# Layer 0 of a four-layer hybrid network: token transposes and affinity logits in one 100-column product per tile, copies interleaved with the norms

## The reference

```
x = x + L0_conv(gn(x))            # super-token attention, the subject here
x = x + L1_conv(gn(x))            # 6-head attention, head mixing, softmax, norm
t = tokens(x)
t = t + L2_attn(ln(t)); t = t + L2_ffn(ln(t))
t = t + L3_attn(ln(t)); t = t + L3_ffn(ln(t))    # four experts, top 2
```

```
stf = blocks.mean(axis=(3, 5))                      # super tokens: mean of a block
s9  = unfold9(stf)                                  # 9 neighbours, missing ones are 0
affinity = softmax(einsum('bnpc,bnck->bnpk', pix, s9) * C**-0.5)
s   = einsum('bnpc,bnpk->bnck', pix, affinity)
stf = fold9(s) / (aff_sum + 1e-12)                  # attention over stf, then out = s9 * affinity
```

## Time and profile before

| | |
|---|---|
| median of three runs | 793.6 us (792.63 to 794.2) |
| the profiled execution | 793.93 us, its span 791.8 us |
| PE, weight loads | 736.5 us busy (93%), 577.3 us (73%) |
| DVE, ACT, GpSimd | 580.7 us (73%), 570.9 us (72%), 252.8 us (32%) |
| chain that ended last | PE 74%, DVE 13%, ACT 4%, issue 4% |
| granted TensorE clock | mean 0.981 |
| DMA | 41.36 MB, mean 52 GB/s |

### The profile page before, as it was taken

One profiled execution on the slowest core, in us unless ns is written; L12 is line 12 of the kernel. 1 busy time (PEld: TensorE's weight loads), 2 busy tenths in 40 slices (PEclk: granted clock), 3 DMA queues, 4 the chain that ended last, 5 costly groups with the idle time before them and its releaser, 6 DMA issues.

```text
span 791.8 us, 16975 instructions
## 1 busy us (share of the span) xinstructions
PE 736.5 (93%) x5269; PEld 577.3 (73%) x5269; DVE 580.7 (73%) x1425; ACT 570.9 (72%) x1427; POOL 252.8 (32%) x485
## 2 busy tenths in 40 slices
PE   1899999999999889999998986999999999999997
PEld 1876878778788776777776585777777787777775
DVE  6245887767677566788886798688888836988885
ACT  2326777787777558888886866788888847777775
POOL 1902345556554432121212000121212111534434
PEclk9999999999999999999999999999999979999999
DMA  6000001011011132233330002233333102233220
GB/s 221 0 2 0 2 12 16 16 22 16 16 21 16 27 91 81 80 101 98 84 104 13 0 1 82 58 94 90 99 99 83 38 1 67 67 72 70 60 50 21
DMA packets 60073, 41.36 MB, mean 52 GB/s; under 512 B 33904, under 2 KB 52464, under 8 KB 59888
## 3 DMA queue, kind: packets, MB, share of 16 engines
q1 hardware_dynamic: 60016, 40.63, 20.3%
HBM read 12.24 MB, written 3.21 MB: 20 GB/s over the span
## 4 chain that ended last, share of the span: by engine, by line
PE 74%; DVE 13%; ACT 4%; issue 4%; DMA 2%; SPq 1%; POOL 1%; POOLq 0%; DVEq 0%
PE ps L1261 11%; PE ps L995 9%; PE ps L1443 9%; PE ps L1186 9%; PE ps L1096 6%; PE ps L1000 5%; PE ps L1080 3%; PE ps L1024 3%; PE ps L1038 2%; PE ps L1003 2%; PE ps L1025 2%; PE ps L945 2%; DVE amax L1902 2%; ACT ee L627 2%; PE ps L1068 2%
## 5 line engine op out<-in xcount | busy, mean ns | idle before, releaser
L627 ACT ACTIVATE ee<-ps,nmax 128x128 f32<-128x128 f32 (+1 forms) x576 | 204.6, 443 | 10.4 <-DVE nmax L1614 5.2
L1261 PE MATMUL ps<-w,ee 128*128 128x128 f32 x960 | 134.6, 273 | 2.0 <-ACT big L614 1.9
L1261 PEld LDWEIGHTS ps<-w,ee 128*128 128x128 f32 x960 | 112.2, 142 | 13.0 <-ACT ee L627 2.8
L614 ACT ACTIVATE big<-ps 128x512 f32<-128x512 f32 (+1 forms) x192 | 96.5, 555 | 22.3 <-PE ps L1261 20.6
L1617 DVE TENSOR_REDUCE nmax<-ps 128x2 f32<-128x256 f32 x192 | 97.4, 549 | 12.2 <-PE ps L1003 7.5
L1745 DVE TENSOR_TENSOR hhl<-ee,hhl 128x512 fp32r<-128x512 f32 x96 | 77.3, 814 | 26.3 <-ACT hhl L864 24.8
L995 PE MATMUL ps<-kh,big 128*128 128x256 f32 x384 | 92.9, 385 | 1.6 <-POOL big L387 1.2
L1614 DVE TENSOR_REDUCE nmax<-ps 128x4 f32<-128x1024 f32 x48 | 58.7, 1223 | 40.9 <-PE ps L995 40.8
L1443 PE MATMUL ps<-hhl,w2hl 128*96 128x512 f32 x288 | 83.3, 399 | 2.1 <-issue 1.8
L1186 PE MATMUL ps<-qk,w1hl 128*128 128x512 f32 x288 | 84.4, 402 | 0.0
L531 POOL TENSOR_TENSOR xc<-big,xc 96x512 f32<-96x512 f32 x32 | 53.0, 1657 | 95.7 <-DVE big L1987 95.2
(11 more groups left out here) (260 smaller groups left out, 1329.2 us busy)
## 6 DMA issues: line engine op xcount, KB each, us to landing
qk<-hl SPq DMA_DIRECT2D x256, 96.0 KB, 3.1
big<-moe_gate SPq DMA_DIRECT2D x8, 768.0 KB, 6.8
w<-w_in SPq DMA_DIRECT2D x1, 1735.0 KB, 12.1
xc<-x_in SPq DMA_DIRECT2D x4, 384.0 KB, 5.6
l_mix<-on SPq DMA_DIRECT2D x32, 48.0 KB, 2.1
tok<-l_mix SPq DMA_DIRECT2D x16, 96.0 KB, 2.0
out<-xc SPq DMA_DIRECT2D x8, 192.0 KB, 2.1
w<-w_in SPq DMA_DIRECT2D x1, 998.0 KB, 8.8
```

Source lines behind the costliest of these rows:

```text
L614: nc.scalar.activation(et[:, h, 0:w], ps[:, 4 + hh, 0:w], ACT.Copy).then_inc(own(l, f"et{hh}"), 1)
L627: last = nc.scalar.activation(ee[:, ke, hh, qc, 0:w], src, ACT.Exp, bias=nmax[:, kp, hh, qc:qc + 1])
L1261: last = nc.tensor.transpose(ps[:, 4 + hh, b * P:(b + 1) * P], ee[:, u, hh, qc, tc * P:(tc + 1) * P], ident)
```

## The change

The moving operand of a tile's product becomes a new buffer `idst`, which holds for each image 4 columns of `stf` and the 96 x 96 identity. One product of 100 columns (ordinary, no longer a transpose) gives logits and tokens side by side, and `l0_xt` holds for each tile a zero column, 4 logits, 96 channels and the one (102 columns for 97).

- ACT writes the 16 copies of the identity into `idst` in one instruction, ahead of `norm_root`; DVE's last step on the means writes the other columns.
- PE waits for both before its first tile, and runs the eight groups in a row; the 32 logit products are gone. Behind the groups stand 20 fills.
- ACT does copies 0 to 3 behind norms 9, 11, 13 and 15 (counted from 0) and copies 4 to 7 behind them; the exponentials come behind all copies.
- DVE waits for all eight copies. The maximum runs over 5 columns, the zero among them, in SBUF, so the maximum with 0 is gone; the subtraction reads the logits from SBUF.
- GpSimd writes the zero column, and its wait for `stf` moves behind the fifth of the nine memsets.

```diff
-            nc.gpsimd.memset(l0_xt[:, :, C:C + 1], 1.0).then_inc(sg("pool_ones"), 1)
+            nc.gpsimd.memset(l0_xt[:, :, 0:1], 0.0).then_inc(sg("l0_zero"), 1)
+            nc.gpsimd.memset(l0_xt[:, :, xw - 1:xw], 1.0).then_inc(sg("pool_ones"), 1)
...
-            pool.wait_ge(sg("l0_dve"), L0_DVE["l0_stf"])
...
                 pool.wait_ge(sg("zeroed"), START + n)
+                if n == 5:
+                    pool.wait_ge(sg("l0_dve"), L0_DVE["l0_stf"])
                 nc.gpsimd.memset(t, 0.0).then_inc(sg("zeroed"), 1)
...
+            act.wait_ge(sg("w128_loaded"), 16)
+            nc.scalar.activation(idst[:, :, M:M + C], mid_dim(wb("ident", C)[:, 0:C], 1, B), ACT.Copy).then_inc(sg("l0_idst"), 1)
             norm_root("gn0", C, 0, B)
...
             for i in range(B):
                 norm_image("gn0", i)
...
-            for g in range(2):
+                if i >= 9 and i % 2 == 1:
+                    tokens_to_sbuf((i - 9) // 2)
+            for g in range(4, 8):
                 tokens_to_sbuf(g)
             act.wait_ge(sg("l0_dve"), L0_DVE["l0_logit"])
...
-            for g in range(2, 8):
-                tokens_to_sbuf(g)
...
-                    last = nc.tensor.transpose(ps[:, 4 + g % 4, t * C:(t + 1) * C], xn[0:C, a:a + P], wb("ident", C)[:, 0:C])
+                    last = mm(ps[:, 4 + g % 4, t * (M + C):(t + 1) * (M + C)], xn[0:C, a:a + P], idst[:, (g * 4 + t) // TPI, :], start=True, stop=True)
...
-            for g in range(2):
+            pe.wait_ge(sg("l0_idst"), 1)
+            pe.wait_ge(sg("l0_dve"), L0_DVE["l0_stf"])
+            for g in range(8):
                 tokens(g)
-            pe.wait_ge(sg("l0_dve"), L0_DVE["l0_stf"])
-            for t in range(NT):
-                i = t // TPI
-                pe.wait_ge(sg("gn0_xn"), i + 1)
-                last = mm(ps[:, 1, t * M:(t + 1) * M], xn[0:C, t * P:(t + 1) * P], stf[:, i * M:(i + 1) * M], start=True, stop=True)
-            last.then_inc(sg("l0_ps"), 1)
-            for g in range(2, 8):
-                tokens(g)
+            fill(20)
...
-            dve.wait_ge(sg("l0_ps"), L0_PS["l0_logit_ps"])
-            lg = ps[:, 1, 0:NT * M].rearrange("p (t m) -> p t m", m=M)
-            link(V.tensor_reduce(out=st[:, 4, :], in_=lg, axis=AX.X, op=ALU.max))
-            link(V.tensor_scalar(st[:, 4, :], st[:, 4, :], 0.0, None, ALU.max))
-            V.tensor_tensor(a0[:, :, :], lg, last_dim(st[:, 4, :], M), ALU.subtract).then_inc(sg("l0_dve"), 1)
+            dve.wait_ge(sg("l0_xt"), 8)
+            dve.wait_ge(sg("l0_zero"), 1)
+            link(V.tensor_reduce(out=st[:, 4, :], in_=l0_xt[:, :, 0:1 + M], axis=AX.X, op=ALU.max))
+            V.tensor_tensor(a0[:, :, :], l0_xt[:, :, 1:1 + M], last_dim(st[:, 4, :], M), ALU.subtract).then_inc(sg("l0_dve"), 1)
```

More of the change, by code:

```diff
@@ L65 @@
 SUMS_AT = {"gn0": 0, "gn1a": 1, "gn1b": 7, "gn1c": 7}
-L0_PS = {"l0_logit_ps": 1, "l0_stok_ps": 2, "l0_stokt_ps": 3, "l0_qkv_ps": 4, "l0_sc_ps": 5, "l0_proj_ps": 6}
+L0_PS = {"l0_stok_ps": 1, "l0_stokt_ps": 2, "l0_qkv_ps": 3, "l0_sc_ps": 4, "l0_proj_ps": 5}
 L0_DVE = {"l0_stf": 1, "l0_logit": 2, "l0_bd": 3, "l0_stok": 4, "l0_stf1": 5, "l0_prod": 6, "l0_sc": 7, "l0_o": 8}
@@ L196, in hybrid_kernel @@
         bd_w = 2 * M * B + M
-        xt_w = NT * (C + 1)
-        l0_xt = big[:, 0:xt_w].rearrange("p (t c) -> p t c", c=C + 1)
+        xw = 1 + M + C + 1
+        xt_w = NT * xw
+        l0_xt = big[:, 0:xt_w].rearrange("p (t c) -> p t c", c=xw)
         l0_bd = big[:, xt_w:xt_w + B * bd_w]
         l0_at = big[0:B * M, xt_w + B * bd_w:xt_w + B * bd_w + B * N]
+        idst_at = xt_w + B * bd_w + B * N
+        idst = big[0:C, idst_at:idst_at + B * (M + C)].rearrange("p (i c) -> p i c", c=M + C)
         rowsum = sb("rowsum", [C, B * N // SB])
@@ L578, in _ @@
             nc.scalar.preload_act_table_set("natural_log_exp_and_others")
+            act.wait_ge(sg("w128_loaded"), 16)
+            nc.scalar.activation(idst[:, :, M:M + C], mid_dim(wb("ident", C)[:, 0:C], 1, B), ACT.Copy).then_inc(sg("l0_idst"), 1)
             norm_root("gn0", C, 0, B)
-            for i in range(B):
-                norm_image("gn0", i)
             def tokens_to_sbuf(g):
                 act.wait_ge(sg("l0_xt_ps"), g + 1)
-                nc.scalar.activation(l0_xt[:, g * 4:(g + 1) * 4, 0:C], ps[:, 4 + g % 4, 0:4 * C].rearrange("p (t c) -> p t c", c=C),
+                nc.scalar.activation(l0_xt[:, g * 4:(g + 1) * 4, 1:xw - 1], ps[:, 4 + g % 4, 0:4 * (M + C)].rearrange("p (t c) -> p t c", c=M + C),
                                      ACT.Copy).then_inc(sg("l0_xt"), 1)
@@ L592, in affinities_to_sbuf @@
                 nc.scalar.activation(l0_at[:, g * 512:(g + 1) * 512], ps[0:B * M, 4 + g % 4, :], ACT.Copy).then_inc(sg("l0_at"), 1)
-            for g in range(2):
+            for i in range(B):
+                norm_image("gn0", i)
+                if i >= 9 and i % 2 == 1:
+                    tokens_to_sbuf((i - 9) // 2)
+            for g in range(4, 8):
                 tokens_to_sbuf(g)
@@ L954, in _ @@
                     pe.wait_ge(sg("l0_xt"), t // 4 + 1)
-                last = mm(ps[0:B * M, 3, 0:C + 1], l0_bd[:, t * B * M:(t + 1) * B * M], l0_xt[:, t, :], start=(t == 0), stop=(t == NT - 1))
+                last = mm(ps[0:B * M, 3, 0:C + 1], l0_bd[:, t * B * M:(t + 1) * B * M], l0_xt[:, t, 1 + M:xw], start=(t == 0), stop=(t == NT - 1))
             last.then_inc(sg("l0_ps"), 1)
@@ L1545, in _ @@
             link(V.tensor_tensor(stf_i, stf_i, last_dim(st[0:C, 5, 0:B], M), ALU.mult))
-            V.scalar_tensor_tensor(out=stf_i, in0=stf_i, scalar=1.0 / (SB * SB), in1=last_dim(st[0:C, 6, 0:B], M), op0=ALU.mult,
+            V.scalar_tensor_tensor(out=idst[:, :, 0:M], in0=stf_i, scalar=1.0 / (SB * SB), in1=last_dim(st[0:C, 6, 0:B], M), op0=ALU.mult,
                                    op1=ALU.add).then_inc(sg("l0_dve"), 1)
-            dve.wait_ge(sg("l0_ps"), L0_PS["l0_logit_ps"])
-            lg = ps[:, 1, 0:NT * M].rearrange("p (t m) -> p t m", m=M)
-            link(V.tensor_reduce(out=st[:, 4, :], in_=lg, axis=AX.X, op=ALU.max))
-            link(V.tensor_scalar(st[:, 4, :], st[:, 4, :], 0.0, None, ALU.max))
-            V.tensor_tensor(a0[:, :, :], lg, last_dim(st[:, 4, :], M), ALU.subtract).then_inc(sg("l0_dve"), 1)
+            dve.wait_ge(sg("l0_xt"), 8)
+            dve.wait_ge(sg("l0_zero"), 1)
+            link(V.tensor_reduce(out=st[:, 4, :], in_=l0_xt[:, :, 0:1 + M], axis=AX.X, op=ALU.max))
+            V.tensor_tensor(a0[:, :, :], l0_xt[:, :, 1:1 + M], last_dim(st[:, 4, :], M), ALU.subtract).then_inc(sg("l0_dve"), 1)
             dve.wait_ge(sg("l0_act"), L0_ACT["l0_exp"])
```

## The result

The changed kernel takes 788.53 us (median of 20 runs, 786.3 to 793.25) against 793.15 for the kernel before, run beside it (median of 20, 790.57 to 795.43): ratio 0.9949, 95% interval 0.9938 to 0.9960, 4.6 us less. The forecast was 784.9, 8.7 us less than the 793.6 then known. The sign was right and the time lies in the range, but the gain is half of what was said.

The account below looks back on a forecast made before the run. Bound: layer 0's single-file chain of waits up to 45.76 us. Copies' end 28.85, + 2.4 DVE, + 0.1 casts, + 5.5 super-token product = 36.9, 8.9 less, shaded to 8.7 off 793.6: 784.9 us; range 783.0 to 790.0.

Parts of the forecast that it names:

- The price of the products: Layer 0's 32 merged products on PE: 0.43 us each at the low clock, 0.223 at the high, set by weights.
- The rise of the clock: During layer 0's merged products: PE's clock rises at 22.3 to 26 us, taken as 23.3.
- L955: Super-token product on PE, last in the stage: 5.5 us at the high clock level, for 6.57 before.
- the formula: End of layer 0's copies: 17.64 us plus 0.481 times the clock's rise time; 28.85 for a rise at 23.3.
- DVE's part: DVE steps between copies and super-token product: L1552 and its 3.12 us gone, that product may start 2.4 us after the copies.
- The cast: GpSimd's two casts beside DVE's last steps: hold them 0 to 0.5 us, taken as 0.1.
- ACT's part: ACT's identity copy, 16 norms and 8 copies: identity copy delays norm_root 0 to 0.1 us, copies done by 27.7.
- Fills: Twenty PE fills behind the products: end near 30.7 us, before the quotient at 31.35, hidden behind ACT and DVE.
- (a): Rival: merged products don't raise the clock; 789.7 to 791.7 us, L955 ending near 42 if fills raise it; chance 0.10.
- (b): Rival: clock falls again between fills and L955, costing 1.1 to 4.9 us: 786 to 789.8 us; chance 0.09.
- (c): Rival: clock stays low until past L955, kernel slower than before at 796 to 799 us; chance 0.03.
- (d): Rival: early GpSimd memsets block bn_stats or its neighbours, up to 6.5 us: 785 to 791.4 us; chance 0.04.

Follow-up runs that it names:

- both edits: Changed kernel with 24 fills ahead of the means and products of 128 columns instead of 100: 781.71 us, ratio 0.9852.

## Why the prediction was right or wrong

**The price of the products was right.** 0.43 and 0.223 us a product were taken from rows 7; the runs have 13.95/32 = 0.436 at the low level and 7.36/32 = 0.230 at the high one. Columns beyond four cost nothing, nor do 128 instead of 100 (7.38 us for the 64 records with both edits).

**The rise of the clock was wrong, and it is the step that failed.** "Products start at 19.07 without a gap, so the earliest rise is 22.3 to 22.7": of the three rises it was read from, none was brought about by products like these. The one near 41.3 came in L955, which has 64 columns of weights and 128 rows; the two later ones came in stretches with 512-column products among them. The first of these was also read as "3.6 us after 37.68", that is, with 1.5 us of transposes counted in; the run with GpSimd's order alone shows 4.08 us of such transposes without a rise. The second stands 3.4 and not 3.2 us behind its drop, which is at 290.5 by the spacing of the records. The 96-column products at 289.5 ran at the high level but had come into it raised. The prediction took keeping a level for raising it. Three profiles of the changed products, unraised, show 13.95 us each; the run with fills ahead shows the same products keeping the level, and the runs with 128 columns or 128 rows show what a little more does. Put the rise back and the sum holds: with 128 columns the copies end within 0.2 us of the formula. The term was 34.06 - 28.85 = 5.2 us too small, part of it the start, 0.5 later in this profile. With 0.5 for the overrun of the fills and the 0.1 for the casts taken off, the sum's 36.9 becomes the measured 42.5.

That the time still lies in the range is in part luck. The stage alone gave 3.7 us, which is 793.15 - 3.7 = 789.5, just under the upper end of 790.0; the rest of the 4.6 lies outside the stage.

**DVE's part was right.** From the end of the copies to the end of the quotient it is 34.06 to 36.46, 2.4 us as said, and the run with GpSimd's order alone shows that the 3.11 us were a wait for the memset. What that is worth by itself was not 3.1 but 2.0 us, as the transposes stood next in line; the change takes these out of the way too. The memsets at 3.9 to 11.6 beside bn_stats did nothing: 8 of them take 2.83 us (5.74 for 16 before). Behind the exponentials of the kernel before stand six token copies (five at 37.06, one at 39.23), not five; no term rests on it.

**The cast was right to 0.1 us, but not met.** In the changed kernel the casts are over at 31.70, before DVE's first step at 34.09. A cast beside these steps shows in the run with 128 columns, timeline of all engines:

```profile
29.90 0.95 POOL L376 MEMSET big<- 32x1024 f32 x1
30.12 0.29 DVE L1554 TENSOR_TENSOR a<-big,st 128x128 f32<-128x128 f32 x1
...
30.92 0.29 POOL L379 CAST identb<-w 128x128 bf16<-128x128 f32 x1
31.15 0.29 POOL L380 CAST maskb<-w 128x128 bf16<-128x128 f32 x1
31.23 0.26 DVE L1557 SCALAR_TENSOR_TENSOR st<-st 128x32 f32<-128x32 f32 x1
```

L1557, with two SBUF inputs, takes 0.26 for 0.19 us beside a cast; L1554, with two as well, keeps its 0.29 us beside a memset. By the rule of the Trainium skill ("SBUF — State Buffer", the two separate sides) the first should suffer and the second not; both rows agree. The hold is small: when L1557 starts, 0.21 us of the second cast are left, and it is 0.07 us longer.

**ACT's part was right and did not matter.** The copy of the identity takes 1.48 us from 11.58, well before norm_root at 15.32. With the clock up, ACT's copies end 27.20 - 15.75 = 11.45 us after the first norm, where 27.7 - 15.57 = 12.1 was said.

**Fills.** "They hide behind ACT and DVE" holds at the high level (0.8 us of wait left in the run with fills ahead), and fails at the low one, as rival (a) had it: 0.5 and 1.3 us past the quotient.

**L955 was right.** 5.56 us for 5.5, once the fills had raised the level.

**The rivals.** (a) is what happened, products slow and the fills raising the clock: L955 "ends near 42", it ended at 42.49. Its 10% were too few; "L945's 13.8 us" was the stronger piece of evidence, since the new stream has the same pace and the same weights. Its times were 1 to 3 us too high: the timed gain of 4.6 is larger than the stage's in either profile of the changed kernel (3.7, and 26.6 - 23.7 = 2.9 in the second). Where the rest comes from is not settled; the level of the clock further on moves by more than that from profile to profile. (b) did not happen in the changed kernel, but the run with fills ahead and none behind shows its mechanism and its price, 17.3 - 15.85 = 1.4 us. The Trainium skill ("TensorE: Matmul & The Clock Gate", Part 4) has it that transposes don't count as work for the clock; in the run with fills ahead only transposes stand between the group averages and the products, and the products are fast from the first, so the trace is against it. (c) and (d) did not happen.

## What to carry to other kernels

Ask of a PE stage that starts after a wait at which level it will start, and whether its own instructions can raise it: compare its pace in the trace (the distance of records) with the same form elsewhere, and take as evidence for a rise only stretches of the same form that began low. Idle PE time ahead of such a stage is the place for fills; here 24 of them took the changed kernel from 788.5 to 783.0 us, 5.5 less, where the rewrite of the stage had brought 4.6 by itself. And of a stall that is taken away, look up what stands next in line before booking its whole length.

## What was not expected of the hardware

- 64 records of 96 rows by 100 columns, 128 columns of weights, run 13.95 us at 1.2 GHz without a rise in three profiles, and keep 2.4 GHz for 7.4 us if they come into it. With 128 columns the rise comes after 5.3 us, with 128 rows after 4.0. One profile stands for each of the two, with timed runs that agree, and which quantity is behind them stays open.
- 4-column products let the level fall at 24.5 in one run, 5 us after the first of them, and near 22.3 in another, 2.6 us after; idleness did so after 2.6 us (29.0).
- With 24 fills ahead the level rose before they ended in two runs (4.32 and 4.49 us for all) and near their end in three (5.02 to 5.16); 24 token transposes, with 96 rows and 96 moving columns, ran 4.08 us without a rise.
- The granted-clock column reads 1.00 from the start until the first change on record, while durations show 1.2 GHz; after that it follows them.
- Timed runs of one kernel spread by 2.7 to 7.6 us here (786.3 to 793.25 for the changed one), and between the profiles of the kernel before and the changed one 2.5 us arose in the gate stage, with the level of the clock.
